# Adapter attention with the second pass 26 steps behind the first, pv at the head of the step, and shift rows sent in two transfers a batch

## The reference, cut to what matters

```
q, k, v = heads(x @ Wq), heads(x @ Wk), heads(x @ Wv)        # 32 heads of 8
q, k    = rope(q), rope(k)
w       = softmax(q @ k.T / sqrt(8) + mask)                   # own keys
a_k, a_v = heads(ctx @ Wk), heads(ctx @ Wv)
a       = tanh(gate) * softmax(q @ a_k.T / sqrt(8))           # adapter keys
x       = layernorm(x + (w @ v + a @ a_v) @ Wo)
```

## Time and profile before

| | |
|---|---|
| Time, median of 3 runs | 1193.47 us (1193.44 to 1193.86) |
| Span of the profiled execution | 1193.7 us |
| TensorE busy | 1128.8 us (95%) |
| VectorE busy | 993.6 us (83%) |
| ScalarE busy | 660.4 us (55%) |
| GpSimd busy | 656.9 us (55%) |
| First pass of stage B (L547 from, L554 to) | 175.6 to 524.4 us |
| Second pass of stage B (L589) | 222.5 to 557.1 us |

### The profile page before, as it was taken

The page is one execution under the profiler, slowest core; times in us unless marked ns, Lnnn a source line. Parts: engine busy times, 40 slices in busy tenths (PEclk is TensorE's granted clock), DMA queues, the critical chain, the costliest instruction groups (busy, mean ns, idle before and its releaser), DMA issues.

```text
span 1193.7 us, 29551 instructions
## 1 busy us (share of the span) xinstructions
PE 1128.8 (95%) x11172; PEld 934.4 (78%) x11172; DVE 993.6 (83%) x2284; ACT 660.4 (55%) x1687; POOL 656.9 (55%) x706
## 2 busy tenths in 40 slices
PE   5899999899999999879999999999999999999997
PEld 5667666666776766546899899998999899997887
DVE  6768887888889898978888888888888888877977
ACT  5466554566766667565555444444444444558663
POOL 4467655545455455254778544544554454847665
PEclk9899999999999999999999999999999999999999
DMA  6875443334333433212222000000000100101111
GB/s 161 205 186 135 122 125 87 87 95 116 88 106 101 106 97 97 76 58 76 68 63 63 1 1 2 1 1 2 1 1 1 37 1 1 37 18 37 36 36 36
DMA packets 98670, 76.68 MB, mean 64 GB/s; under 512 B 73547, under 2 KB 86987, under 8 KB 98529
## 3 DMA queue, kind: packets, MB, share of 16 engines
q1 hardware_dynamic: 98529, 74.80, 23.1%
HBM read 53.86 MB, written 19.92 MB: 62 GB/s over the span
## 4 chain that ended last, share of the span: by engine, by line
PE 58%; DVE 23%; issue 7%; ACT 5%; POOL 3%; SPq 2%; DMA 2%; DVEq 0%; POOLq 0%; ACTq 0%
PE bank L1518 5%; DVE B_nr L737 4%; PE bank L1519 4%; PE bank L1520 4%; PE bank L1574 4%; PE bank L1547 4%; PE bank L611 4%; DVE PT L746 3%; PE bank L472 2%; PE bank L554 2%; SPq L1154 2%; PE bank L1534 2%; PE bank L1589 2%; PE bank L1587 2%; PE bank L1588 2%
## 5 line engine op out<-in xcount | busy, mean ns | idle before, releaser
L1822 POOL TENSOR_TENSOR C_QK<-C_t1b,C_t2b 128x512 f32<-128x512 f32 x128 | 168.9, 1320 | 226.6 <-DVE C_t2b L1661 226.0
L1658 DVE SCALAR_TENSOR_TENSOR C_t1b<-bank,C_bcol,C_tabs 64x512 f32<-64x512 f32 x256 | 192.0, 750 | 37.3 <-PE bank L1520 33.2
L737 DVE TENSOR_REDUCE B_nr<-bank 128x4 f32<-128x512 f32 x256 | 164.4, 684 | 22.6 <-PE bank L554 21.0
L1518 PE MATMUL bank<-C_XTh,C_Wh 128*128 128x512 f32 x256 | 111.9, 437 | 4.4 <-DVE C_t2b L1661 1.9
L985 ACT ACTIVATE PT<-bank 128x512 f32<-128x512 f32 x160 | 92.2, 598 | 39.8 <-PE bank L589 39.3
L1754 ACT ACTIVATE C_P<-bank,C_nm 128x128 f32<-128x128 f32 x256 | 90.7, 367 | 34.0 <-DVE C_nm L1671 32.4
L978 ACT ACTIVATE PT<-PT 128x512 f32<-128x512 f32 x96 | 59.3, 630 | 88.7 <-DVE PT L746 88.7
L1773 ACT ACTIVATE C_V<-bank 128x512 f32<-128x512 f32 x64 | 38.1, 597 | 124.1 <-PE bank L1536 122.5
L611 PE MATMUL bank<-PT,vpool 128*32 128x128 f32 x2048 | 97.4, 285 | 4.3 <-ACT PT L978 3.1
L1519 PE MATMUL bank<-C_XTl,C_Wh 128*128 128x512 f32 x256 | 101.2, 395 | 0.0
L1520 PE MATMUL bank<-C_XTh,C_Wl 128*128 128x512 f32 x256 | 100.8, 394 | 0.0
(11 more groups left out here) (267 smaller groups left out, 3683.5 us busy)
## 6 DMA issues: line engine op xcount, KB each, us to landing
Adrq<-PB SPq DMA_DIRECT2D x16, 192.0 KB, 3.2
Adrk<-PB SPq DMA_DIRECT2D x16, 192.0 KB, 3.4
stk<-Adrq SPq DMA_DIRECT2D x16, 192.0 KB
stk<-Adrk SPq DMA_DIRECT2D x16, 192.0 KB
Bdrq<-PB SPq DMA_DIRECT2D x16, 192.0 KB, 2.7
stk<-Bdrq SPq DMA_DIRECT2D x32, 96.0 KB
Bdrk<-PB SPq DMA_DIRECT2D x16, 192.0 KB, 2.7
stk<-Bdrk SPq DMA_DIRECT2D x32, 96.0 KB
```

The source lines that it names most:

```text
L737: e.tensor_reduce(dst, bank[n % 2][:, :].rearrange("p (a b) -> p a b", a=4), AX.X, ALU.max, negate=True).then_inc(sem("m_dve"), 1)
L1518: e.matmul(o[:, :], CWh[hp][:, cs], XCh[0][:, t, :], start=t == 0, stop=False)
L1658: e.scalar_tensor_tensor(out=v4(t1b[kq][lo:lo + 64, :]), in0=v4(o[hi:hi + 64, :]), scalar=bc[hi:hi + 64, :], in1=tabsC[hi:hi + 64, 2 * kq ...
L1822: e.tensor_tensor(QK[v % 3][:, kq, :], t1b[kq][:, :], t2b[kq][:, :], ALU.add).then_inc(sem("rc_pool"), 1)
```

## The change

Four things change together, and the diff is whole but for its context:

- The second pass of stage B comes 26 steps behind the first one, not 28. In stage A it stays 12 behind. The first unit with four banks is 294, not 292.
- pv stays in the step in which it was (30 behind the first pass in stage B, 14 in stage A), so it is now four steps behind the second pass in stage B. From step 64 on it is the first work of TensorE in a step.
- The buffer of split maxima is laid out with the half of the heads outermost, and the transposes give, for each half, the rows of both kinds one after the other.
- So SyncE sends for each half of the heads one transfer with the six rows of both kinds, two a batch in place of four, and the semaphore counts 32 a batch, not 64.

```diff
-    LAST_FIRST = 292
+    LAST_FIRST = 294
...
     def shift_sem(g):
-        return (f"shift_A{g % 4}", 16 * (g // 4 + 1)) if g < 16 else (f"shift_B{g % 2}", 64 * ((g - 16) // 2 + 1))
+        return (f"shift_A{g % 4}", 16 * (g // 4 + 1)) if g < 16 else (f"shift_B{g % 2}", 32 * ((g - 16) // 2 + 1))
...
     def pass2_units(s):
-        return [s - 12] if 12 <= s < NA + 12 else pair(s - 28)
+        return [s - 12] if 12 <= s < NA + 12 else pair(s - 26)
 
     def pv_units(s):
-        return pass2_units(s - 2)
-
-    STEPS = NN + 28 + 2 + 12
+        return [s - 14] if 14 <= s < NA + 14 else pair(s - 30)
+
+    STEPS = NN + 30 + 12
...
-        heads = lambda a: a[:, :, :].rearrange("p k (g h) -> p k g h", h=16)
+        heads = lambda a: a[:, :, :].rearrange("p k (g h) -> p g k h", h=16)
...
-            for kd in range(NK[L]):
-                m = e.transpose(gv[0:3 * NH[L], kd * 128:kd * 128 + 128], nmb[L][:, kd, :, :, :].rearrange("p g a b -> p (g a b)"), identb[:, :])
+            for hg in range(1 + L):
+                m = e.transpose(gv[0:48 * NK[L], hg * 128:hg * 128 + 128], nmb[L][:, hg, :, :, :].rearrange("p k a h -> p (k a h)"), identb[:, :])
...
         for s in steps:
+            if s >= NA:
+                for n in pv_units(s):
+                    pv(n)
             if pass1_units(s):
                 pass1(pass1_units(s))
             if pass2_units(s):
                 pass2(pass2_units(s))
-            for n in pv_units(s):
-                pv(n)
+            if s < NA:
+                for n in pv_units(s):
+                    pv(n)
...
-            e.activation(nmT[L][g % 2][:, :, :].rearrange("p a b -> p (a b)"), home["sh", g][:, :].bitcast(BF16)[0:3 * nh, 0:nk * 128],
+            e.activation(nmT[L][g % 2][:, :, :].rearrange("p a b -> p (a b)"), home["sh", g][:, :].bitcast(BF16)[0:48 * nk, 0:128 * (1 + L)],
                          ACT.Copy).then_inc(sem("sh_act"), 1)
...
             for hg in range(1 + L):
-                for kd in range(NK[L]):
-                    row = 64 * hg + 48 + 3 * kd if L else 96
-                    load(QS[L][b % (5 if L else 10)][row:row + 3, :, :], nmT[L][b % 2][48 * hg:48 * hg + 48, kd, :],
-                         shift_sem(g)[0])
+                row = 64 * hg + 48 if L else 96
+                load(QS[L][b % (5 if L else 10)][row:row + 3 * NK[L], :, :], nmT[L][b % 2][:, hg, :], shift_sem(g)[0])
```

More of the change, by code:

```diff
@@ L966, in shift @@
             L = g // 16
-            nk, nh = NK[L], NH[L]
+            nk = NK[L]
             q.wait_ge("sh_pe", g + 1)
```

## The result

The changed kernel takes 1208.19 us (median of four executions) beside 1193.55 (1193.44 to 1193.86) for the kernel before on the same chip: ratio 1.0111, 95% interval 1.0092 to 1.0130. Three of the four took 1205.88 to 1208.36 us at a mean granted clock of 0.986 to 0.989; the fourth took 1376.18 at 0.748, has no trace, and is left out of the ratio. The kernel is 1.1% slower where 0.4% was forecast.

A forecast was written before the change was run, and what follows sets the result against it. The prediction took a tight exchange between TensorE and VectorE as the bound. Steady batches +5.4, start +0.8 and tail -1.5 gave +4.7 us on 1193.47: 1198.2 us, 0.4% slower, range 1190.0 to 1203.5.

The forecast's parts named there:

- P7 to P2 take up the other 0.5: Even batch: pair steps P7 to P2 (of eight, P0 to P7) absorb lateness of P6's second pass, costing 0 us.
- (b): Pair step P2: second pass starts sooner after its first pass once P1 loses its mask additions; 0.18 us back.
- (a): P1's exponentials no longer wait for mask additions; VectorE's 0.67 us wait for L1084 goes, 0.2 us counted through to L746.
- Pv first: TensorE's ring of work keeps its length with pv last in it: 0, besides 0.9 us once from waits on exponentials.
- Shift rows: P5's reader just meets two merged transfers: 0, bounds 0 and +0.5 a batch; four would land too late.
- R3: Rival, rows late: merged transfers cost double to issue, land 1.5 us later for P5's reader; 1203.7 us, chance 0.04.
- R1: Rival, absorbed: one pair's buffer between the engines takes up P5's mask additions; period +0.3, 1194 us, chance 0.20.
- R2: Rival, faster: the chain ScalarE L926, GpSimd, L1084, VectorE sets the pace from P1 to P5; 1188.3 us, chance 0.24.
- Start: Start of stage B's second passes: that of step 92 waits for mask additions; +0.8 us, bounds 0 and 1.2.
- How many periods: Between start and tail: six odd and seven even batches, 6 x 0.9 = +5.4 us.
- Tail: Stage B's end into stage C: pv stops waiting for exponentials, rope comes sooner; -1.5 us, bounds -4 and +1.
- Sum: Whole kernel: +5.4, +0.8 and -1.5 give +4.7 us; nothing lies around the span, so 1198.2 us, chance 0.52.

The follow-up runs named there:

- the two reductions: Two VectorE reductions that nobody reads, added to the changed kernel: behind P5's mask additions 1220.39 us, ratio 1.0219; behind P1's maxima 1205.84 us, ratio 1.0104.

## Why the prediction was wrong in size

The direction and the place were right. What failed in the changed kernel is the step "P7 to P2 take up the other 0.5" in the even batch, with the 0.2 of (b) in the odd one, and with it the view that a batch has one budget of idle time: from P6 to P3 a period was to get back 0.76 us and lost 0.36 more. The starts of the second passes of P3 and P6, in us, from the traces:

| stretch | before | after | forecast | lag alone |
|---|---|---|---|---|
| P3 to P6, even | 7.36 | 7.90 (+0.54) | +0.56 | 8.36 (+1.00) |
| P6 even to P3 odd | 14.27 | 14.34 (+0.07) | -0.56 | 13.76 (-0.51) |
| P3 to P6, odd | 7.02 | 7.91 (+0.89) | +1.1 | 8.36 (+1.34) |
| P6 odd to P3 even | 14.46 | 14.75 (+0.29) | -0.2 | 14.25 (-0.21) |
| period | 43.10 | 44.90 (+1.80) | +0.9 | 44.73 (+1.63) |

Up to P6 the sum held within about 0.2 us. The last column sets a limit to this account. With the lag alone the stretches behind P6 did give back 0.51 and 0.21 us, as forecast, and there it was the lateness at P6 that was too small in the sum: 1.00 and 1.34 us, not 0.56 and 1.1. pv at the head makes P3 to P6 shorter by 0.46 and 0.45 and the rest longer by 0.58 and 0.50. So where the loss shows depends on the order, and its size hardly does. That the row of VectorE is full prices this size in one line: 1.28 us is added ahead of P6's maxima, and only the idle time that stood before these, 0.61 in the even batch and 0.23 in the odd one, could take it up. 0.67 + 1.05 = 1.72 us, against 1.63 measured for the lag alone. By stretches the sum is made up otherwise (2.65 from P5 to P0, and 1.02 given back from P0 to P5), so the line fits the total and is not shown to be its cause. VectorE's row in the kernel before, odd batch, P6:

```profile
437.77 1.29 DVE L737 TENSOR_REDUCE B_nr<-bank 128x4 f32<-128x512 f32 x2 [0.23 <-PE bank L554]
438.98 1.28 DVE L746 TENSOR_TENSOR PT<-bank,stk 128x512 f32<-128x512 f32 x2
```

I had used that 0.61 in the even batch twice: once as the reason why L746 would end only 0.76 late, and again as room to catch up. The Trainium skill ("Perfetto Trace Analysis", section "Optimization Strategy") says that the most contended engine can change over time within a kernel; the two reductions agree, with 0.83 us a batch in P5 and 0 in P1, at a grain of a few pair steps. And the 1.2 us that left P1 I looked for on ScalarE's chain only. It fell into a stretch where TensorE is 98% busy, and the stretch became only 0.42 and 0.34 us shorter.

Point by point:
- *(a) and (b).* The wait for L1084 went, and P4 to P5 became shorter by 0.36 us in the even batch (2.29 to 1.93 from first pass to first pass) and by 0.30 in the odd one. So (a) is somewhat larger than my 0.2. But only half of it comes from where I took it, L746 leaving P1: with the lag alone VectorE's waits for L1084 fall from ten (6.1 us) to five (3.3), P4 to P5 is 0.31 us shorter in the odd batch and as long as before in the even one (2.27), and the rest came with pv first. (b): the second pass of P2 does start 0.23 behind its first pass in both batches, instead of 0.40, but from P2 to P3 it is 2.83 us as before, so it gave nothing. With the lag alone that step is 2.64, 0.19 shorter in both batches.
- *Pv first, "the same length, 0".* With the lag it costs 0.15 us a period, the small difference of the two shifts above. The transposed input's bank used to be emptied while pv ran; now the small products wait for that in P5, 0.45 us in each batch:

```profile
421.91 0.39 PE L472 MATMUL bank<-XTh,B_Wh 128*128 128x256 f32 x1 [0.46 <-DVE XTl L727]
```

- *Shift rows.* No reader waits for them with two transfers, as forecast. "The merging is needed for the lag" was wrong: with four the readers wait 5.8 us in all, hidden behind P6's wait. R3 did not happen. The 2.84 us from issue to reader was the wrong row: in place it is 2.1, so that P5's reader had about 0.7 more room than the sum gave it. The Trainium skill ("DMA: Bandwidth & Descriptors", section "Anatomy of one DMA") gives its fixed cost of some 2.0 us for transfers that GpSimd issues. These go by SyncE, and the 2.1 of the lag alone lies near it.
- *Rivals.* R1 (absorbed) rested on slack in P5 to P7 that isn't there. R2's chain (faster) is real, but P4 to P5 gained 0.3 to 0.36 us a batch, not 0.6, and in the even batch not because L746 left P1.
- *Start.* Forecast +0.8; the first two batches of stage B take 53.88 us instead of 51.50, +2.4. 0.84 of it lies in the first batch, before any second pass of stage B: from its P0 to the next it is 31.96 us instead of 31.12, and so it is in every kernel with pv first, while every one with pv last has 31.1. So this belongs to the order, which I had at 0. The other 1.54 lie in P6 of the second batch (5.22 us instead of 3.68), the step that I had priced at 0.85. TensorE's clock was down for a part of it in both kernels (granted 0.67 after and 0.54 before), so that the lag's part is not separate here; with the lag alone that batch is 0.75 us longer. In the kernel before with merged transfers, where the clock stayed up, the step takes 2.19 us.
- *How many periods.* I took six from start to tail. Batches 2 to 13 give +9.7 us (1.91, 1.74, 1.75, 1.80, 1.80 and 0.69) and the last two up to their last first pass +1.9. In these two the clock has a part. Behind waits of 1.12 us for mask additions it fell in both steps from P6 to P7, which take 3.89 and 4.49 us instead of 2.04 and 2.05; with pv last, after the same waits and at full clock, they take 3.34. TensorE's windows (the clock is the third figure from the end):

```profile
510.42:514.31 3.89, 2.76 (x38) 0.83 0.09 26
531.72:536.21 4.49, 3.37 (x38) 0.69 0.19 58
```

- *Tail.* Forecast -1.5, and from the last first pass to the end it is 1204.1 - 536.21 = 667.9 us instead of 1193.7 - 523.97 = 669.7: -1.8. It is made up differently. "They don't" was wrong: a pv product still waits 1.23 us for exponentials, and the transpose 1.76 instead of 0.33:

```profile
540.82 0.28 PE L565 MATMUL bank<-identb,B_nmb 128*96 128x128 bf16 x2 [1.76 <-ACT C_XF L1495]
...
543.24 0.43 PE L611 MATMUL bank<-PT,vpool 128*32 128x128 f32 x8 [1.23 <-ACT PT L982]
```

  The second pass ends 4.5 us sooner after the last first pass, and stage C takes 2.6 us longer from there. Where in stage C wasn't followed up. The ends of both kernels, before and after:

```profile
523.97 0.40 PE L554 MATMUL bank<-stk 48*128 48x128 bf16 x8
...
556.71 0.40 PE L589 MATMUL bank<-stk 54*128 54x128 bf16 x8
```

```profile
536.21 0.61 PE L554 MATMUL bank<-stk 48*128 48x128 bf16 x8
...
564.48 0.40 PE L589 MATMUL bank<-stk 54*128 54x128 bf16 x8
```

- *Sum.* -1.7 (stage A reached stage B that much sooner in this execution) + 2.4 + 9.7 + 1.9 - 1.8 = +10.5, and the spans differ by 10.4. The medians differ by 14.6. Of the rest 1.8 is that the profiled execution's time, 1205.88, is that much above its span. I had said that nothing lies around the span, because the 1193.7 of the earlier trace rows is so near the median; but that span is from an execution of its own, and where time and span of one execution of the kernel before are both known, the time is longer by 1.8 too (1192.15 and 1190.3). The other 2.3 is the distance from that execution to the median of the changed kernel. The range's upper end, 1203.5, stood for a period at +1.8, and the period came out there: the 4.7 us beyond it are, but for 0.1, these 4.2 outside the spans, 1.6 at the start and 0.8 in the last batches, less 1.7 of stage A and 0.3 of the tail.

Shown by runs: that the lag makes the loss, that merging gives nothing, that VectorE's time costs in P5 and is free in P1, and that moving the second pass of P6 does not help. Only argued: the one-line price of 1.72, which fits but was tried at one size of the load only, and why pv first shifts the loss from one stretch to the other. Not tried: a lag of 28 with pv two pairs behind, and VectorE's sums of z (L805 and what follows, 1.2 us in P6) moved out of the full row.

## What to carry over

Where two engines exchange banks, don't ask how much idle time a period has, but in which steps each engine has it, and cut the period into the stretches that each one sets. Work moved from a stretch that the other engine sets into one that its own engine sets can cost its whole length there (here 2.56 us a period) and give back little where it came from (here 0.76). A small dummy load in either place, 1 us long, says which stretch is whose more surely than the waits do; and before a waiting instruction is moved behind "independent" work, follow who empties that work's banks.

## What the hardware showed that I had not expected

- pv at the head of the step one pair after its second pass cost 14.6%: not a wait or two, but a chain through TensorE, VectorE and ScalarE in four of a batch's eight steps, and TensorE's granted clock was lower with it, a mean of 0.83 over the window of 130 us in which TensorE was busy for 103.9.
- In the steady part of the order with pv last, TensorE waited four times for 1.12 or 1.13 us in the odd batch's P6. In three of these steps the clock fell to its lower level (1.2 instead of 2.4 GHz) for a part of the step, which took 6.1 to 6.3 us instead of 4.8 (granted clock 0.72 over the window shown above), in the fourth it did not, nor in any of the four such steps (waits of 0.97 to 1.13 us) of the kernel with the lag alone. In the last two batches it is the other way round: behind waits of 1.12 and 1.13 us the clock stayed up with pv last, and behind 1.13 and 1.05 us it fell with the lag alone (granted 0.83 and 0.59 over the steps). So the length of the wait alone does not tell.
- A load of 1.0 us on an engine that is busy 85% of a period (38.0 of 44.9 us) cost 0.83 us in one step and 0.00 in another, four steps away.
